# Pointwise stage: the one-channel image spread for four tiles at once; depthwise stage: padded lines, another order of places, longer stores

## The reference

```python
# layer 2: c1 is a 3x3 convolution to one channel, c2 a product with one 128x128 matrix
t = relu(c1(x)); y = concat([x[:, :1], x[:, 1:] + t[:, :-1]])
u = relu(c1(y)); z = u + roll(y, 1, axis=1)          # apart from the last two rows
v = relu(c2(z)); p = concat([z[:, :, :1], z[:, :, 1:] + v[:, :, :-1]])
r = relu(c2(p)); q = r + roll(p, 1, axis=2)          # apart from the last two columns
# layer 3, B and gate_B depthwise 7x7, A the same at every position but the kernel's own
gate_A, gate_B = sigmoid(conv(gate_A_kernel, x)), sigmoid(conv(gate_B_kernel, x))
a, b = A * gate_A, conv(B_kernel, x) * gate_B
# T = 8 steps of h = (1 - sigmoid(a)) h + sigmoid(a) (softplus(b) + 1e-6)
out = h @ W_out + b_out
```

## Time and profile before

| | us |
|---|---|
| median of three runs | 4745.81 |
| lowest, highest | 4656.36, 4747.08 |
| the profiled execution | 4665.72 |
| its span (first to last instruction) | 4663.7 |

### The profile page before, as it was taken

The page is one execution under the profiler, slowest core; times in us unless marked ns, Lnnn a source line. Parts: engine busy times, 40 slices in busy tenths (PEclk is TensorE's granted clock), DMA queues, the critical chain, the costliest instruction groups (busy, mean ns, idle before and its releaser), DMA issues. The chain is left out here.

```text
span 4663.7 us, 108212 instructions
## 1 busy us (share of the span) xinstructions
PE 4324.7 (93%) x35238; PEld 3310.7 (71%) x35238; DVE 3407.1 (73%) x10109; ACT 2858.4 (61%) x7950; POOL 2102.6 (45%) x1792
## 2 busy tenths in 40 slices
PE   5999999999999999877999989999739997999995
PEld 5777777777777777646677757777414447999995
DVE  7888888888888888663666656666339993667665
ACT  0888888888888888513333333333317882666664
POOL 0777777777777777513233313333016650222222
PEclk8999999999999999899999989999869998999997
DMA  7222222222222222385222222221847887999994
GB/s 317 69 77 77 80 77 79 78 76 80 77 76 80 77 77 80 130 292 183 68 73 71 72 83 71 73 71 64 301 164 254 295 279 254 278 286 294 288 294 113
DMA packets 726507, 679.49 MB, mean 146 GB/s; under 512 B 59029, under 2 KB 609172, under 8 KB 717399
## 3 DMA queue, kind: packets, MB, share of 16 engines
q1 hardware_dynamic: 710507, 643.38, 45.0%
q10 hardware_dynamic: 11645, 15.81, 1.0%
q0 software_dynamic: 3808, 13.47, 0.7%
HBM read 473.14 MB, written 199.29 MB: 144 GB/s over the span
## 5 line engine op out<-in xcount | busy, mean ns | idle before, releaser
L325 POOL TENSOR_TENSOR at_bias<-at_tri,at_mask 128x1024 f32<-128x1024 f32 x512 | 1204.6, 2375 | 115.7 <-DMA at_mask<-in_L_conv_mask_bias_dram 111.1
L465 ACT ACTIVATE at_probs<-at_neg_s,at_neg_max 128x256 f32<-128x256 f32 x2048 | 1012.9, 504 | 0.5 <-DVE at_neg_max L509 0.5
L509 DVE CUSTOM_DVE_ANT_0 at_neg_s<-at_p_s,at_bias 128x256 f32<-128x256 f32 x2048 | 761.9, 419 | 17.9 <-PE at_p_s L367 3.6
L1008 ACT ACTIVATE ml_h<-ml_p_turns,l_b 128x512 f32<-128x512 f32 x384 | 263.9, 687 | 608.1 <-PE ml_p_turns L967 608.1
L380 PE MATMUL at_p_t<-all_ident,at_probs 128*128 128x128 f32 x4096 | 614.1, 273 | 1.1 <-DVE at_probs_t L517 0.6
L976 PEld LDWEIGHTS ml_p<-l_w1s,ml_h 128*128 128x128 f32 x4096 | 471.9, 192 | 52.7 <-issue 52.7
L380 PEld LDWEIGHTS at_p_t<-all_ident,at_probs 128*128 128x128 f32 x4096 | 487.3, 141 | 28.3 <-ACT at_probs L465 2.6
L967 PE MATMUL ml_p_turns<-ml_h,l_w 128*128 128x512 f32 x1024 | 486.2, 598 | 2.3 <-DVE ml_h L1041 2.3
L976 PE MATMUL ml_p<-l_w1s,ml_h 128*128 128x128 f32 x4096 | 484.6, 277 | 0.8 <-issue 0.8
L1109 POOL TENSOR_TENSOR ml_x2t<-ml_z,ml_xb 128x512 f32<-128x512 f32 x128 | 163.3, 1276 | 678.3 <-DVE ml_z L1075 678.3
L2036 POOL TENSOR_TENSOR dw_room<-dw_room,all_b_plain 128x512 f32<-128x512 f32 x128 | 175.6, 1372 | 598.5 <-DMA dw_room<-x3t 598.5
(11 more groups left out here) (232 smaller groups left out, 9225.7 us busy)
## 6 DMA issues: line engine op xcount, KB each, us to landing
dw_xw<-planes SPq DMA_DIRECT2D x128, 528.0 KB, 4.7
dw_wts<-patch_w SPq DMA_DIRECT2D x128, 512.0 KB, 6.0
planes<-pw_plane SPq DMA_DIRECT2D x128, 264.0 KB, 3.1
in_xs<-in_x_dram SPq DMA_DIRECT2D x32, 1024.0 KB, 7.7
at_xs<-in_x_dram SPq DMA_DIRECT2D x256, 128.0 KB, 2.3
at_kvs<-in_L_conv_kv_x_dram SPq DMA_DIRECT2D x256, 128.0 KB, 2.3
at_mask<-in_L_conv_mask_bias_dram SPq DMA_DIRECT2D x256, 128.0 KB, 3.2
x<-at_x1s SPq DMA_DIRECT2D x256, 128.0 KB, 1.8
```

The source lines that it names most:

```text
L325: pool.tensor_tensor(bias[:, n % 2, part], tri[:, part], mask[:, n % 4].unsqueeze(1).broadcast_to((128, 4, COLS)), ALU.add).then_inc(maske ...
L465: e = act.activation(probs[:, h, qh, :], neg_s[:, n % 2, h, qh, :], ACT.Exp, bias=neg_max[:, n % 2, i:i + 1], scale=-1.0, accum_out=sums[: ...
L509: t = dve.tensor_tensor_reduce(neg_s[:, n % 2, h, qh, :], p_s[h][:, qh, :], bias[:, n % 2, i, :], -1.0, 3.0e38, ALU.add, ALU.min, neg_max[ ...
L1008: act.activation(h1[:, b, :], bank_of(hidden_use(t, b))[:, :], ACT.Relu, bias=b0[:, b:b + 1]).then_inc(relu_act, 1)
```

## The change

Patch weights: `ox, oy` where there was `oy, ox`, so that the 64 spots are ordered by x first.

Pointwise: the spread runs for four tiles every four steps, in row groups at partitions 0, 32, 64 and 96, into four banks. `p_v` and `p_n` have one bank each in exchange. The second product stands ahead of the transposes in TensorE's list. Loads are issued two tiles earlier.

Depthwise: a line of `raw` has four elements more (528 bytes). The transposes write their 128 columns as 32 runs of four, 16 elements apart, so that four patches interleave; `hid` is ordered [spot group, patch, four rows]. Softplus runs in two halves that write runs of 16. A partition of the result now is a patch column and one of four rows, and its four pieces are four positions across: one store of 128 partitions with 2 KB runs, where there were four. The residual is loaded in four transfers as before, each over all partitions.

```diff
@@ spread_taps
-                    oy, ox = divmod(spot + i, PATCH)
+                    ox, oy = divmod(spot + i, PATCH)
@@ pointwise_part
-        ones = m.sb("ones", [33, 128])
+        ones = m.sb("ones", [97, 128])
-        taus = m.sb("taus", [33, 4, 2, COLS])
+        taus = m.sb("taus", [97, 2, 2, COLS])
-        p_v = [m.ps(f"p_v{i}", [128, 2, COLS]) for i in range(2)]
+        p_v = m.ps("p_v", [128, 2, COLS])
-        p_n = [m.ps(f"p_n{i}", [128, 4, CH]) for i in range(2)]
-        p_tau = [m.ps(f"p_tau{i}", [128, 2, COLS]) for i in range(2)]
+        p_n = m.ps("p_n", [128, 4, CH])
+        p_tau = [m.ps(f"p_tau{i}", [128, 2, COLS]) for i in range(4)]
@@ SP
-                if 0 <= t + 6 < tiles and t + 6 >= 4:
-                    load(t + 6)
+                if 5 <= t + 8 < tiles:
+                    load(t + 8)
@@ TensorE
-                    if a >= 2:
-                        pe.wait_ge(p_made, a - 1)
-                    pe.matmul(p_v[a % 2][:, :, 1:COLS], w[:, :], z[:, a % 4, :, 0:COLS - 1],
+                    if a >= 1:
+                        pe.wait_ge(p_made, a)
+                    pe.matmul(p_v[:, :, 1:COLS], w[:, :], z[:, a % 4, :, 0:COLS - 1],
                               start=True, stop=True).then_inc(v_mul, 1)
...
                     pe.matmul(p_r[t % 2][:, :, 0:COLS - 1], w[:, :], p[:, t % 2, :, 0:COLS - 1],
                               start=True, stop=True).then_inc(r_mul, 1)
-                if 0 <= h < tiles and h % 2 == 0:
...
+                if 0 <= e < chunks:
+                    g = e // 8
+                    pe.wait_ge(x3_made, 8 * g + 8)
+                    pe.wait_ge(x3_wrapped, g + 1)
+                    if e >= 1:
+                        pe.wait_ge(plane_read, e)
+                    for j in range(4):
+                        mm = pe.transpose(p_n[:, j, :], x3b[:, g % 2, e % 8 * 4 + j].rearrange("p y d -> p (y d)"), ident[:, :])
+                    mm.then_inc(x3_turned, 1)
+                if 0 <= h < tiles and h % 4 == 0:
+                    for i in range(4):
+                        pe.wait_ge(loaded[(h + i) % 8], h // 8 * 32 + 32)
                     pe.wait_ge(z_made, h)
-                    for i in range(2):
+                    for i in range(4):
@@ depthwise_layer
-        raw = m.sb("raw", [128, CH, BLOCK_PY * PX])
+        raw = m.sb("raw", [128, CH, BLOCK_PY * PX + 4])
-        hid = m.sb("hid", [128, 2, SPOTS, PX])
+        hid = m.sb("hid", [128, 2, SPOTS // 4, PX, 4])
-        p_turn = [m.ps(f"p_turn{i}", [128, PATCH, 2 * SPOTS]) for i in range(2)]
+        p_turn = [m.ps(f"p_turn{i}", [128, 2, 2, SPOTS // 4, 4, 4]) for i in range(2)]
@@ load_residual, store
-                    sp.dma_start(xr[d * PX:(d + 1) * PX, w % 4], cells[(1 - x) * SHIFT + d][:, y:y + 4]).then_inc(r_loaded[w % 4], 16)
+                    sp.dma_start(xr[:, w % 4, d], cells[(1 - x) * SHIFT + d][:, y:y + 4]).then_inc(r_loaded[w % 4], 16)
...
-                for d in range(4):
-                    sp.dma_start(out[0, r * PATCH + y:r * PATCH + y + 4].rearrange("y (a d) c -> d a y c", d=PATCH)[x + d],
-                                 outs[d * PX:(d + 1) * PX, w % 4]).then_inc(stored[w % 4], 16)
+                cells = out[0, r * PATCH + y:r * PATCH + y + 4].rearrange("y (a d) c -> a y d c", d=PATCH)
+                sp.dma_start(cells[:, :, x:x + 4].rearrange("a y d c -> a y (d c)"),
+                             outs[:, w % 4].rearrange("p d c -> p (d c)")).then_inc(stored[w % 4], 16)
@@ turn
-                    cells = raw[:, patch, :] if u // units % 2 else raw[:, :, patch]
-                    mm = pe.transpose(p_turn[u % 2][:, i, :], cells, ident[:, :])
+                    cells = raw[:, patch, 0:CH] if u // units % 2 else raw[:, :, patch]
+                    places = p_turn[u % 2][:, i // 4, :, :, i % 4].rearrange("p f s y -> p (f s) y")
+                    mm = pe.transpose(places, cells, ident[:, :])
@@ softplus
-                dve.scalar_tensor_tensor(out=hid[:, r % 2, :, x:x + PATCH].rearrange("p s a -> p a s"), in0=bt[:, u % 3],
-                                         scalar=0.0, in1=soft[:, u % 2], op0=ALU.max, op1=ALU.add).then_inc(hid_made, 1)
+                for half in range(2):
+                    part, at = slice(half * BANK // 2, (half + 1) * BANK // 2), x + half * 4
+                    done = dve.scalar_tensor_tensor(out=hid[:, r % 2, :, at:at + 4].rearrange("p s a y -> p s (a y)"),
+                                                    in0=bt[:, u % 3, part].rearrange("p (s n) -> p s n", n=16), scalar=0.0,
+                                                    in1=soft[:, u % 2, part].rearrange("p (s n) -> p s n", n=16),
+                                                    op0=ALU.max, op1=ALU.add)
+                done.then_inc(hid_made, 1)
```

More of the change, by code:

```diff
@@ L1497, in load @@
                     sp.dma_start(xs[:, 2 * slot + 1:2 * slot + 3], rows[:, g * 2:g * 2 + 2]).then_inc(loaded[slot], 16)
-                at = g % 2 * 32
-                sp.dma_start(taus[at:at + 1, slot // 2].rearrange("p r w -> p (r w)"),
+                at = g % 4 * 32
+                sp.dma_start(taus[at:at + 1, slot // 4].rearrange("p r w -> p (r w)"),
                              tau.rearrange("(g n) -> g n", n=2 * COLS)[g:g + 1]).then_inc(loaded[slot], 16)
-            for n in range(4):
+            for n in range(5):
                 load(n)
             for t in steps:
-                if 0 <= t + 6 < tiles and t + 6 >= 4:
-                    load(t + 6)
+                if 5 <= t + 8 < tiles:
+                    load(t + 8)
                 e = t - 10
@@ L1618, in _ @@
                         act.wait_ge(tokens_stored[e % 4], token_stores(e))
-                    act.activation(x3n[:, e % 4], p_n[e % 2][:, :, :], ACT.Copy).then_inc(tokens_read, 1)
+                    act.activation(x3n[:, e % 4], p_n[:, :, :], ACT.Copy).then_inc(tokens_read, 1)
                     if e % 8 == 0 and g >= 2:
                         act.wait_ge(planes_stored[g % 2], plane_stores(g % 2, g))
-                    act.activation(plane[:, g % 2, :, px:px + 4], p_n[e % 2][:, :, :].rearrange("p a c -> p c a"),
+                    act.activation(plane[:, g % 2, :, px:px + 4], p_n[:, :, :].rearrange("p a c -> p c a"),
                                    ACT.Copy).then_inc(plane_read, 1)
@@ L1626, in _ @@
         def _(dve):
+            dve.memset(p_v[:, :, 0:1], LOWEST)
             for i in range(2):
-                dve.memset(p_v[i][:, :, 0:1], LOWEST)
                 done = dve.memset(p_r[i][:, :, COLS - 1:COLS], 0.0)
@@ L1649, in _ @@
                     dve.wait_ge(z_made, t + 1)
-                    dve.scalar_tensor_tensor(out=p[:, s], in0=p_v[s][:, :, :], scalar=low, in1=z[:, t % 4],
+                    dve.scalar_tensor_tensor(out=p[:, s], in0=p_v[:, :, :], scalar=low, in1=z[:, t % 4],
                                              op0=ALU.max, op1=ALU.add).then_inc(p_made, 1)
@@ L1733, in depthwise_layer @@
         f_shift = m.sb("f_shift", [128, 2])
-        hid = m.sb("hid", [128, 2, SPOTS, PX])
+        hid = m.sb("hid", [128, 2, SPOTS // 4, PX, 4])
         room = m.sb("room", [128, 15, BANK])
-        gate, bt, soft = (room[:, a:z].rearrange("p n (a s) -> p n a s", s=SPOTS) for a, z in ((0, 2), (2, 5), (5, 7)))
+        gate, bt, soft = (room[:, a:z] for a, z in ((0, 2), (2, 5), (5, 7)))
         xr, outs = (room[:, a:z].rearrange("p n (a c) -> p n a c", c=CH) for a, z in ((7, 11), (11, 15)))
         p_conv = [m.ps(f"p_conv{i}", [128, 4, BLOCK_PY * PX]) for i in range(2)]
-        p_turn = [m.ps(f"p_turn{i}", [128, PATCH, 2 * SPOTS]) for i in range(2)]
+        p_turn = [m.ps(f"p_turn{i}", [128, 2, 2, SPOTS // 4, 4, 4]) for i in range(2)]
+        by_patch = [t[:, :, :, :, :, :].rearrange("p h f s a y -> p h f (s a y)") for t in p_turn]
+        og_turn = by_patch[0].rearrange("p h f n -> p (h f n)")[:, 0:2 * CH].rearrange("p (a n) -> p a n", a=2)
         p_out = [m.ps(f"p_out{i}", [128, 4, CH]) for i in range(2)]
@@ L1752, in depthwise_layer @@
         og_final = m.sb("og_final", [KTAPS, CH])
-        og_room = hid[:, :, :, :].rearrange("p r s a -> p (r s a)")
+        og_room = hid[:, :, :, :, :].rearrange("p r s a y -> p (r s a y)")
         og_taken = 0
@@ L1892, in turn_origin @@
                 for i in range(2):
-                    mm = pe.transpose(p_turn[0][:, i, :], og_xs[:, i, :], ident[:, :])
+                    mm = pe.transpose(og_turn[:, i, :], og_xs[:, i, :], ident[:, :])
                 mm.then_inc(og_turned, 1)
@@ L1925, in copy_raw @@
             else:
-                done = copy(raw[:, c:c + 4, :], p_conv[g % 2][:, :, :])
+                done = copy(raw[:, c:c + 4, 0:BLOCK_PY * PX], p_conv[g % 2][:, :, :])
             done.then_inc(copied, 1)
@@ L2090, in origin_window @@
                     chained(dve.tensor_copy(og_win[:, :, first:first + k],
```

(2 more changed lines are left out.)

35 lines of the change are left out of this document (12 added, 23 removed).

## The result

The changed kernel takes 4701.2 us (median of four runs, 4698.1 to 4776.5). The ratio to the kernel before, run beside it, is 1.0093, 95% interval 1.0063 to 1.0122: some 43 us slower. The two profiled executions are 4698.1 and 4665.7 us, and their spans 4696.0 and 4663.7: +32.3 us.

What follows compares the result with a forecast made beforehand. TensorE's queue was taken to set the pointwise step (2.79 us) and to be full in depthwise. Terms +41 - 19 - 2 - 11 = +9 us on the median of 4745.8 gave about 4755, range 4630 to 4800.

Steps and rivals of the forecast that it cites:

- +41 for pointwise: Pointwise as a whole: slower by 41 us, between -33 and +55.
- The chain, +37: Pointwise steps: a loop across TensorE, VectorE and ScalarE closes, 3.13 us a step instead of 2.82, +37 us over 119 steps.
- The end of pointwise, +4: Last nine chunks of pointwise: transposes wait for both copies, 1.94 us each instead of 1.02; +4 us, between 0 and +8.
- Rival A: Pointwise: the loop doesn't close, VectorE sets the step, -26 us there, 58 us faster with depthwise's -32; chance 0.26.
- the bounds for pointwise: Pointwise: from -33 us (step at VectorE's 2.57, 128 x 0.25) to +55.
- Four row groups in the time of two: Pointwise spread: four tiles side by side cost 1.26 us with going in and out, the same as two.
- Lines, -19: Depthwise blocks reading columns: 528-byte pitch cuts units from 5.63 to 5.34 us, -19 us, between 0 and -19.
- rival C: Depthwise: the longer pitch does nothing, +28 us in all instead of +9, 4774 us; chance 0.22.
- Softplus: Depthwise: two halves at 0.37 us each for 1097 ns, hidden in the plateau, -2 us in the last 16 units.
- The stores, -11: Depthwise's end: five store issues take 2.4 us instead of 9.71, -7, and about -4 before them; 0 in the plateau.
- The signs: What would confirm or refute: pointwise step, TensorE's share and clock, late loads, depthwise units of 5.34 or 5.63, last stretch 93 us.

Runs made afterwards that it cites:

- one-bank kernel: The kernel before with one edit, one bank instead of two for the first product: 4704.7 us, ratio 1.0098 [1.0076, 1.0121].

## Why the prediction was right or wrong

The verdict, within 2%, was right, and so was the main claim: four-tile spreads don't pay, because a chain closes. The sum said +9 and +32 to +43 came, so it was a third of what came, or less; by the profiles, +41 for pointwise became +58, -19 for the lines -12, and -13 for softplus and stores -13. That the range held it owes much to its width of 170 us, taken for both footings, and says little for the sum. The time of 4755 stood on the median of 4745.8 shown then, against 4701.2 now; on the profile's footing the prediction said 4675, and the profiled execution took 4698. Step by step:

**The chain, +37, measured +48.** The links were right to 0.03 but for first to second product, 0.94 for 0.86. The first product's pair of records is 1.09 us there, behind an idle time, and not 1.02; behind a spread, without an idle time, it is 1.12 in both kernels, so why it is longer stays open. So the clean step is 3.17 (12.68 us over four, 3736.90 to 3749.58) and not 3.13: 5 of the 11 us. The others come of the subtraction: I set a clean 3.13 against 2.82, which is a mean over 98 steps with its hiccups. The clean step before was 2.79, as my own text had it, and the mean after is 3.24; 119 x (3.24 - 2.82) = 50. That the order is what closes this chain, the experiments on it show; the prediction began it with the single bank, and it closes with two as well (3.01). What I missed is the second chain, through `p`, first product, spread and `z`, which the one-bank kernel shows at 3.19 a step by itself, with a spread every other step. With a spread every fourth step it is 2.96 (the transposes ahead of the second product), under the 3.17 of the first, so in the changed kernel it isn't the one that sets the step.

**The end of pointwise, +4, measured +9.5.** I took half of a bound of 8. The copies and transposes take turns there as forecast, but 2.42 us apart and not 1.94: the granted clock is 0.60 in the stretch, a mean between the levels of 2.4 and 1.2 GHz, with TensorE busy 13 of 48 us, and four transposes take 1.09 us where the first ones of the stretch still took 0.63. The stretch of before already had 0.67, and I had priced its links from the plateau's rows.

**Rival A** (no chain, -58) is denied by the step and by TensorE at 82%. With the transposes first its mechanism does appear, steps at VectorE's 2.57, but only three in four: the fourth, with the spread's wait and in part one for a store, gives the gain back (2.85 on the mean). Its -26 for pointwise was therefore too good. It also stood on a step of 2.62 us that no row has, where the text ahead of it had 2.57 and 2.6; and in the bounds for pointwise 128 x 0.25 is 32 and not 33, and the +55 has no working.

**Four row groups in the time of two.** 1.14 us against 1.13: right.

**Lines, -19, measured -12; rival C** (nothing) denied. The column turn fell from 1.17 to 0.96 and not to 0.87. I took the far end of my own range without a row for it.

**Softplus.** Alone a pair takes 0.76 us, as priced; beside GpSimd's bias add (L2038) up to 1.87, and two halves take 1.27 on the mean of the plateau (2 x 635 ns), more than the 1.10 of the single one. The rows, here from the changed kernel, show how:

```profile
4400.69 1.26 POOL L2038 TENSOR_TENSOR dw_room<-dw_room,all_b_plain 128x512 f32<-128x512 f32 x1 [4.55 <-DMA dw_room<-x3t]
4401.11 1.47 DVE L2074 SCALAR_TENSOR_TENSOR dw_hid<-dw_room 128x256 f32<-128x256 f32 x2 [1.77 <-ACT dw_room L1967]
```

A softplus that starts during a bias add is lengthened by about what is left of it, less some 0.1 us (1.47 for 0.76, with 0.84 left). One that starts first is not, and the bias add is: in the kernel before, 1.07 and 1.97 us at 4544.54 and 4544.66, where it takes 1.27 alone. Two halves leave it a place to come between. It was hidden, as said.

**The stores, -11.** With softplus -13, and the last stretch fell by 13. The size was right and its parts were not: an issue of 2 KB runs takes 0.88 and not 0.48, so the five took 4.40 and not 2.4, and the four loads went up by 0.7; a unit's loads and store ahead of them came to 3.1 us of issues and not 2.4. The last stores' issues account for 5.3 of the 13 us. Ahead of them TensorE waits 26.8 us in the stretch for VectorE's residual add, where it waited 36.1; one wait behind that (stores freeing a buffer, 10.9) gave way to a shorter one (loads, by way of the bias add, 7.6). No run takes softplus and stores apart here, so that the sum of -13 came out is in part luck.

**The signs.** The clock did not fall in pointwise (0.99), no wait for a load stands among TensorE's there, and the last stretch is 93 us as named; the units of 5.43 us lie between the two that were named.

## What to carry to other kernels

Before a buffer is halved to pay for something, follow each loop that then closes through every in-order queue, those that the change leaves alone too (here ScalarE's), and price both it and the next longest; a change of order in one queue can close such a loop by itself (+29 here with two banks each), or open it, as the transposes put first do. Subtract like from like: a clean period from a clean period, a mean from a mean. For transfers, sum the issues of a unit on the queue that makes them and compare with the unit: a pattern of access can cost there though the bandwidth is idle.

## What the runs showed of the hardware

- Columns of `raw` as a transpose's input: eight in 1.17 us at a pitch of 512 bytes, 1.00 to 1.04 at 516, 0.95 at 520, 0.96 at 528, and 0.87 for lines. Four bytes more cure half of it.
- Steps in the place that a transpose writes to cost nothing (0.96 us with runs of four and with single elements; 1.17 at 512 bytes with runs of four, as before without steps).
- One-row products in four row groups take 1.14 us for four tiles, in two 1.13 for two.
- A DMA of 64 KB in runs of 512 bytes takes SP 0.60 us to issue over all partitions and 0.43 over 32; one of 256 KB in runs of 2 KB takes 0.88 at the end of the kernel and 0.60 in the plateau.
- VectorE's softplus and GpSimd's bias add hold each other up: whichever starts second is lengthened by about what is left of the first (a pair of halves from 0.76 up to 1.87 us, the bias add from 1.27 up to 1.97).
